# Windowed attention on TensorE: two windows' scores in one product, attention and transposes cut into other runs, new orders on all engines

## The chip, the cores and the metric

One core of a Trainium2 chip. The metric is the device time of one execution in microseconds; the median of three runs stands for the kernel. The profile is one further look at one execution.

The engines in the profile's words: PE is TensorE's matmul and PEld its weight load, DVE is VectorE, ACT ScalarE, POOL GpSimd, SPq the queue that issues the DMAs.

## The reference, cut to what matters

A cross attention over x and a context (32 batches of 128 tokens of 128), then a stack of six layers, each with windowed attention and a gated feed-forward. Per layer and batch, in fp32:

```python
qkv = x @ Wqkv                      # 128 x 3072, x with half its features shifted by one token
q, k = l2norm(q) * qs, l2norm(k) * ksc   # 16 heads of 64
q = q * cos * scale + rotate_half(q) * sin * scale
k = k * cos * inv + rotate_half(k) * sin * inv
# 4 windows of 32 queries; window w sees the keys of windows w-1 and w
sim = jnp.where(mask, -big, einsum('bhwie,bhwje->bhwij', bq, bk2) * 8)
out = softmax(sim) @ bv2
x = x + out @ Wo
xn = layernorm(shifted x); a, gate = split(xn @ W1 + b1)
x = x + (a * gelu(gate)) @ W2 + b2
```

## The kernel before, in words

A unit is one batch in one layer: 192 units, numbered layer by layer. The cross attention runs first, in 32 slots of its own (`xslot`). Then each engine runs the same `slot(n, k)` for n = -2, -1, ... 196, most of them in a loop of two slots per pass. In one slot an engine handles parts of several units: `part(n, lag)` gives unit n - lag. The order of the calls at the end of each engine's `slot` is the order in which that engine works; between engines there are only semaphores. So the slots overlap as in a pipeline, and the time of one slot is the time per unit.

TensorE's slot is written out at the end of the kernel: `attn_out` (L1363), `ffn_out` (L1351), a projection of queries and keys (`proj_qk`, L1252), `transpose_qk` (L1290), `transpose_z` (L1377), two projections, `transpose_P` (L1270), `scores` (mask L1314, products L1322), `attend` (L1339), `transpose_zn` (L1383), `proj_v` (L1262), `ffn_gate` (L1392), `ffn_a` (L1400), and two projections of the next and this unit.

Where an operand has fewer than 128 rows or an output fewer than 128 partitions, matmuls use a part of the array, a tile, and several tiles work side by side:

- `transpose_qk`: 64 transposes of 32 tokens x 128 features, four row tiles.
- `transpose_P`: 16 transposes of 64 tokens x 128, two row tiles.
- `scores`: 8 pairs of heads x 4 windows x 2 heads = 64 products of 32 queries with 64 keys (64 rows x 32 columns of the array, 64 columns streamed), on eight tiles (2 by head, 4 by window).
- `attend`: for 4 head groups, three windows of queries (64, 32 and 32 wide), 2 halves and 2 heads: 48 products on four tiles of 64 x 64. Values stand shifted in three copies (`vs`), made by three DMAs per half (`shift_v`).

An fp32 product is two matmul instructions in the trace, each with a weight load; a transpose is one.

ScalarE copies PSUM to SBUF (`copy_T`, `copy_PT`, `copy_o`, `copy_v`), squares the projections, and takes exponentials and gelu, with two table loads a slot. VectorE multiplies by the rotary tables (`rotary`, L963 and L966), sums squares, refines the inverse root, does maximum, subtraction and row sums of the softmax, and the statistics and the normalising step of the layer norm (`norm_apply`, L1030). GpSimd adds the rotary halves, multiplies by the norms and the softmax's factors, and does the layer norm's power. At the first unit of each layer, the new weights are loaded by the same DMA queue that shifts the values and `zm`.

## Time and profile before

| | us |
|---|---|
| median of 3 runs | 3308.11 |
| lowest and highest | 3307.62, 3310.73 |
| span of the profiled execution | 3304.7 |
| TensorE busy | 3125.4 |
| VectorE busy | 2884.0 |
| ScalarE busy | 2663.4 |
| GpSimd busy | 2447.9 |
| TensorE busy in the first 400 us (cross attention and first slots) | 297.3 |
| TensorE busy from 400 to 3200 us | 2750.5 |
| TensorE busy from 3200 us to the end | 77.6 |

The profile counts an engine busy from the start of an instruction to its end, overlapping ones once. The start of a matmul is read from the record, its end is modelled (about 0.22 us after the start in the tiled runs); how long a run of matmuls holds TensorE is therefore read from its first start to the first start of what follows.

### The profile page before, as it was taken

What the parts mean: (1) busy time and instruction counts of PE and PEld (TensorE: products, weight loads), DVE (VectorE), ACT (ScalarE), POOL (GpSimd) and SP (SyncE); (2) the same over time, 40 slices, a digit from 0 to 9 for tenths busy, and PEclk for the clock granted to TensorE, in tenths of its full rate; (3) what the DMA queues carried; (4) which work ended last, traced back from release to release, by engine and by line L of the source; (5) the groups of instructions that cost most, each with busy time, mean ns of one, the idle gap of its engine ahead of it and who ended that gap; (6) DMA issues with size and microseconds to landing.
All of it is one profiled execution on the core that took longest, in us unless ns stands there. A gap on an engine that the chain in (4) does not pass through costs nothing.

```text
span 3304.7 us, 181505 instructions
## 1 busy us (share of the span) xinstructions
PE 3125.4 (95%) x71268; PEld 2192.5 (66%) x71268; DVE 2884.0 (87%) x6045; ACT 2663.4 (81%) x5440; POOL 2447.9 (74%) x2673
## 2 busy tenths in 40 slices
PE   6776899999999999999999999999999999999996
PEld 4443567676667676676767667676676767667665
DVE  7886789999899999899999899998899999899984
ACT  6886678888788888788888788888788888788874
POOL 3333778888788888788888778787787878788883
PEclk9988999999999999999999999999999999999997
DMA  3000112122222222222222212122221212212121
GB/s 79 8 7 10 47 51 59 50 59 71 67 56 53 56 53 77 63 54 55 54 55 74 68 50 59 50 59 77 57 59 50 59 50 77 66 50 59 50 58 50
DMA packets 150374, 182.24 MB, mean 55 GB/s; under 512 B 51572, under 2 KB 74162, under 8 KB 149554
## 3 DMA queue, kind: packets, MB, share of 16 engines
q1 hardware_dynamic: 150322, 181.55, 21.2%
q8 instruction: 33, 0.54, 0.1%
q14 instruction: 19, 0.16, 0.0%
HBM read 21.32 MB, written 2.10 MB: 7 GB/s over the span
## 4 chain that ended last, share of the span: by engine, by line
PE 57%; issue 13%; DVE 10%; ACT 10%; POOL 5%; SPq 1%; DVEq 1%; DMA 1%; ACTq 1%; POOLq 0%
PE bank L1252 13%; PE bank L1339 8%; PE bank L1322 7%; PE bank L1262 5%; PE bank L1363 5%; PE bank L1270 3%; PE bank L1290 3%; ACT L798 3%; DVE tb L966 3%; ACT P L774 3%; PE bank L1392 2%; ACT gl L766 2%; POOL qk L524 2%; DVE bank L1075 2%; PE bank L1400 2%
## 5 line engine op out<-in xcount | busy, mean ns | idle before, releaser
L533 POOL TENSOR_TENSOR qk<-qk,rn 128x512 f32<-128x512 f32 x768 | 803.0, 1046 | 356.8 <-DVE rn L985 356.8
L524 POOL TENSOR_TENSOR qk<-ta,tb 128x512 f32<-128x512 f32 x768 | 978.6, 1274 | 2.5 <-DVE tb L966 2.5
L1252 PE MATMUL bank<-wqkv,zsT 128*128 128x512 f32 x1536 | 819.9, 617 | 25.4 <-ACT vt L705 12.3
L963 DVE TENSOR_TENSOR ta<-bank,rot 128x512 f32<-128x512 f32 x768 | 527.5, 687 | 116.1 <-ACT sq L688 87.4
L966 DVE TENSOR_TENSOR tb<-bank,rot 128x512 f32<-128x512 f32 x768 | 523.0, 681 | 0.0
L1068 DVE TENSOR_REDUCE bank<-sq 128x32 f32<-128x2048 f32 x192 | 440.6, 2295 | 25.1
L688 ACT ACTIVATE sq<-bank 128x512 f32<-128x512 f32 x768 | 445.2, 611 | 14.8 <-PE bank L1252 12.1
L696 ACT ACTIVATE qkT<-bank 128x512 f32<-128x512 f32 x768 | 396.6, 602 | 57.1 <-PE bank L1290 56.9
L1363 PEld LDWEIGHTS bank<-wo,oT 128*128 128x128 f32 x3072 | 375.4, 193 | 92.4 <-issue 92.4
L743 ACT ACTIVATE znT<-bank,small 128x128 f32<-128x128 f32 x192 | 87.9, 458 | 431.8 <-PE bank L1383 431.8
L564 POOL TENSOR_TENSOR P<-P,rowsum 128x512 f32<-128x512 f32 x384 | 392.9, 1045 | 20.0 <-DVE rowsum L1083 20.0
L1262 PE MATMUL bank<-wqkv,zsT 128*128 128x512 f32 x768 | 399.8, 603 | 1.2 <-DVE tb L966 1.1
L1363 PE MATMUL bank<-wo,oT 128*128 128x128 f32 x3072 | 376.6, 276 | 0.5 <-ACT gl L766 0.5
L1252 PEld LDWEIGHTS bank<-wqkv,zsT 128*128 128x128 f32 x1536 | 238.0, 195 | 193.1 <-DVE tb L966 170.2
L1290 PEld LDWEIGHTS bank<-cst,qk 32*128 32x128 f32 x12288 | 212.5, 137 | 172.9 <-issue 172.9
L1339 PE MATMUL bank<-PT,vs 64*64 64x32 f32 (+1 forms) x18432 | 310.9, 220 | 11.3 <-issue 11.3
L1339 PEld LDWEIGHTS bank<-PT,vs 64*64 64x64 f32 x18432 | 291.4, 135 | 30.0 <-issue 12.3
L539 POOL TENSOR_TENSOR rstd<-ve,half_neg 128x1 f32<-128x1 f32 x192 | 105.8, 551 | 254.5 <-DVE ve L1023 254.5
L1075 DVE TENSOR_REDUCE bank<-P 128x16 f32<-128x1024 f32 x192 | 235.8, 1228 | 66.7 <-ACT P L774 66.6
L1322 PEld LDWEIGHTS bank<-qkT 64*32 64x32 f32 x24576 | 278.1, 105 | 14.1 <-issue 3.9
L1322 PE MATMUL bank<-qkT 64*32 64x64 f32 x24576 | 281.7, 225 | 3.0 <-issue 3.0
L1290 PE MATMUL bank<-cst,qk 32*128 32x32 f32 x12288 | 228.5, 223 | 21.0 <-DVE rowsum L1083 2.9
(131 smaller groups left out, 5740.6 us busy)
## 6 DMA issues: line engine op xcount, KB each, us to landing
vs<-vt SPq DMA_DIRECT2D x1152, 128.0 KB, 2.4
wqkv<-L_ffn_Wqkv SPq DMA_DIRECT2D x6, 1024.0 KB, 5.0
zm<-zm SPq DMA_DIRECT2D x192, 31.8 KB
wqkv<-L_ffn_Wqkv SPq DMA_DIRECT2D x6, 512.0 KB, 3.7
wo<-L_ffn_Wo SPq DMA_DIRECT2D x6, 512.0 KB, 4.0
z_sb<-x SPq DMA_DIRECT2D x4, 512.0 KB, 5.1
ctxb<-ctx SPq DMA_DIRECT2D x32, 64.0 KB, 1.8
w<-L_ffn_W SPq DMA_DIRECT2D x6, 341.0 KB
```

Of the source, the lines that this page charges most:

```text
L524: g.tensor_tensor(o, i0, i1, ALU.add).then_inc(s["g_add"], 1)
L533: g.tensor_tensor(q3, q3, r3, ALU.mult).then_inc(s["g_qk"], 1)
L688: a_.activation(sq[:, 512 * j:512 * j + 512], bank[j % 2][:, :], ACT.Square)\
L963: v_.tensor_tensor(ta[:, c].rearrange("p (h d) -> p h d", d=DH), bank[j % 2][:, :].rearrange("p (h d) -> p h d", d=DH), rot[:, o:o + 64].u ...
L966: v_.tensor_tensor(tb[:, c].rearrange("p (h c d) -> p h c d", c=2, d=32)[:, :, ::-1, :], bank[j % 2][:, :].rearrange("p (h c d) -> p h c d ...
L1068: v_.tensor_reduce(sm, sq[:, :].rearrange("p (h d) -> p h d", d=DH), AX.X, ALU.add)\
L1252: t_.matmul(bank[j % 2][:, :], zsT[:, pu, :], wqkv[:, 512 * j:512 * j + 512], start=True, stop=True).then_inc(s["p_qk"], 1)
L1262: t_.matmul(bank[r][:, :], zsT[:, k % 2, :], wv[:, :, r, :], start=True, stop=True)\
L1290: ins = t_.transpose(TB[t][:, 32 * p:32 * p + 32], qk[tok, pb, 128 * p:128 * p + 128], ident[tok, tok])
L1322: ins = t_.matmul(SC[e][32 * w:32 * w + 32, 64 * p:64 * p + 64], qkT[dr, p, 32 * w:32 * w + 32], qkT[dr, PAIRS + p, k0:k0 + 64], start=Fal ...
L1339: ins = t_.matmul(bank[4 + r][64 * e:64 * e + 64, 128 * i + q0:128 * i + q0 + nq], vs[kr, pc, w, hc:hc + 64], PT[kr, 4 * e + i, q0:q0 + nq ...
L1363: ins = t_.matmul(bank[7][:, 384:512], oT[:, p, :], wo[:, 2 * (p % 4) + p // 4, :], start=p == 0, stop=p == PAIRS - 1)
```

## The change

- A product of the scores covers windows 0 and 1 together (64 queries, the same 64 keys) on two tiles; windows 2 and 3 keep 32-query products, on four tiles, with window 2's two halves of keys in reversed order. The mask is widened for that reversed order. 48 products in place of 64.
- The scores run in two parts: mask and windows 2 and 3; later windows 0 and 1.
- Attention times values: two sets of key rows in place of three. One run of 16 products is 96 queries wide, the other 64 wide and adds to the same banks; the transposed weights stand in PTA and PTC, with a factor of 0 or 1 per partition (`C_HALF`) where only half the keys count. 32 products in place of 48. The two runs stand in different slots. `vs` has two copies, so two DMAs per half.
- Queries and keys are transposed in 64-row tiles, in two runs of 16 (keys to banks 2 and 3, queries to banks 4 and 5).
- ScalarE copies the transposed weights in four pieces in place of two.
- The statistics of the norms (`sm`, `n0`, `n1`, `rs`) stand in SBUF in place of PSUM. The layer norm's small add and its normalising step go from VectorE to GpSimd.
- Each engine has a new order of the same parts, with other lags: the projections of queries and keys one slot before the unit's values, scores at lag 1, softmax and attention at 2 and 3, the feed-forward at 4. Each part has a semaphore of its own. Inside the loop only the waits that others don't imply are kept (`edge` waits stand outside the loop alone).

```diff
+    c[:, C_MASK + 64:C_MASK + 96] = c[:, C_MASK + 32:C_MASK + 64]
+    c[:, C_MASK + 96:C_MASK + 128] = c[:, C_MASK:C_MASK + 32]
+    c[:, C_HALF] = (r // WIN) % 2
+    c[:, C_HALF + 1] = 1 - (r // WIN) % 2
...
-        PT = sb("PT", [128, PAIRS, S])
+        PTA = sb("PTA", [128, PAIRS, 3 * WIN])
+        PTC = sb("PTC", [128, PAIRS, 2 * WIN])
         vt = sb("vt", [128, 2, 2, INNER // 2])
-        vs = sb("vs", [128, 2, 3, INNER // 2])
+        vs = sb("vs", [128, 2, 2, INNER // 2])
...
+        sm = sb("sm", [128, 2 * HEADS])
+        n0 = sb("n0", [128, 2 * HEADS])
+        n1 = sb("n1", [128, 2 * HEADS])
+        tiny = sb("tiny", [128, 2 * HEADS])
+        eps = sb("eps", [128, 1])
+        rs = sb("rs", [128, HEADS])
...
+        def done(unit, total=UNITS):
+
+            return min(max(unit + 1, 0), total) if isinstance(unit, int) else unit + 1
+
+        def unit(n, k, lag, total=UNITS):
+
+            u = n - lag
+            return u, (not isinstance(u, int)) or 0 <= u < total, (k - lag) % 2
 
...
+                for r in (0, 1):
+
+                    wait(sp, f"a_v{r}", done(u))
                     wait(sp, "p_AV", count(2, u - 2, 2))
                     rows = slice(64 * r, 64 * r + 64)
-                    for j in range(3):
-                        sp.dma_start(vs[rows, par, j, :], vt[32 * j:32 * j + 64, par, r, :]).then_inc(s[f"l_v{par}"], 16)
+                    for j in range(2):
+                        sp.dma_start(vs[rows, par, j, :], vt[64 * j:64 * j + 64, par, r, :]).then_inc(s[f"l_v{par}"], 16)
...
+                u, on, p = unit(n, k, 3)
+                if on:
+                    wait(pool, "d_agg", done(u))
+                    g.tensor_tensor(ve[:, p:p + 1], mv[:, 1:2], eps[:, 0:1], ALU.add).then_inc(s["g_ve"], 1)
+                    wait(pool, "g_ve", done(u))
+                    g.tensor_tensor(rstd[:, p:p + 1], ve[:, p:p + 1], half_neg[:, 0:1], ALU.pow).then_inc(s["g_rstd"], 1)
+
+                u, on, p = unit(n, k, 3)
+                if on:
+                    wait(pool, "g_rstd", done(u))
+                    edge(pool, u, "p_znT", done(u - 1))
+                    pool.nop(nofuse=True)
+                    g.tensor_scalar(zn[:, :], zm[:, p, 0:2, :].rearrange("p c e -> p (c e)"), mv[:, 0:1], rstd[:, p:p + 1],
+                                    ALU.subtract, ALU.mult).then_inc(s["d_zn"], 1)
+
...
+                    a_.activation(PTA[:, :, 0:64], bank[4][:, :].rearrange("p (h q) -> p h q", h=PAIRS), ACT.Copy).then_inc(s["a_PA0"], 1)
...
+                    a_.activation(PTC[:, :, 0:32], bank[5][:, :].rearrange("p (h q) -> p h q", h=PAIRS)[:, :, 0:32], ACT.Copy, scale=cst[:, C_HALF + 1:C_HALF + 2]).then_inc(s["a_PC0"], 1)
...
+                    a_.activation(PTC[:, :, 32:64], bank[5][:, :].rearrange("p (h q) -> p h q", h=PAIRS)[:, :, 32:64], ACT.Copy).then_inc(s["a_PC1"], 1)
...
+                    a_.activation(PTA[:, :, 64:96], bank[5][:, :].rearrange("p (h q) -> p h q", h=PAIRS)[:, :, 0:32], ACT.Copy, scale=cst[:, C_HALF:C_HALF + 1]).then_inc(s["a_PA1"], 1)
...
-                        for p in range(2 * PAIRS):
-                            for t in range(4):
-                                tok = slice(32 * t, 32 * t + 32)
-                                ins = t_.transpose(TB[t][:, 32 * p:32 * p + 32], qk[tok, pb, 128 * p:128 * p + 128],
-                                                   ident[tok, tok])
-                                if p == 2 * PAIRS - 1:
...
-                            for w, (q0, nq) in enumerate(((0, 64), (64, 32), (96, 32))):
-                                for r in range(2):
-                                    for e in range(2):
-                                        kr = slice(64 * r, 64 * r + 64)
-                                        hc = 128 * i + 64 * e
-                                        ins = t_.matmul(bank[4 + r][64 * e:64 * e + 64, 128 * i + q0:128 * i + q0 + nq],
-                                                        vs[kr, pc, w, hc:hc + 64], PT[kr, 4 * e + i, q0:q0 + nq],
-                                                        start=True, stop=True)
...
-                attn_out()
-                ffn_out()
-                proj_qk(1)
-                transpose_qk()
-                transpose_z()
-                proj_qk(2)
-                proj_qk(3)
-                transpose_P()
-                scores()
-                attend()
-                transpose_zn()
-                proj_v(0)
-                ffn_gate()
-                ffn_a()
-                proj_qk(0)
-                proj_v(1)
...
+                    wait(pe, "p_AV0", done(u))
...
+                    pe.nop(nofuse=True)
+                    for i in range(4):
+                        for r in range(2):
+                            for e in range(2):
+                                kr = slice(64 * r, 64 * r + 64)
+                                hc = 128 * i + 64 * e
+                                ins = t_.matmul(bank[4 + r][64 * e:64 * e + 64, 128 * i + 64:128 * i + 128],
+                                                vs[kr, p, 1, hc:hc + 64], PTC[kr, 4 * e + i, :],
+                                                start=False, stop=True, skip_group_check=True)
+                        if i % 2 == 1:
+                            ins.then_inc(s["p_AV"], 1)
...
+                u, on, p = unit(n, k, 1)
+                if on:
+                    wait(pe, "g_qk2", done(u))
+                    wait(pe, "d_sub1", done(u - 1))
+                    edge(pe, u, "g_qk3", done(u))
+                    edge(pe, u, "d_sub0", done(u - 1))
+                    if isinstance(u, int) and u == 0:
+                        pe.wait_ge(s["x_x1"], B)
+                    pe.nop(nofuse=True)
+                    for c in range(PAIRS):
                         for t in range(2):
                             tok = slice(64 * t, 64 * t + 64)
...
+                            ins = t_.transpose(bank[2 + t][:, 64 * c:64 * c + 64],
+                                               qk[tok, p, 1024 + 128 * c:1152 + 128 * c], ident[tok, tok])
+                    ins.then_inc(s["p_trk"], 1)
...
+                    wait(pe, "g_qk0", done(u))
...
+                    pe.nop(nofuse=True)
+                    for c in range(PAIRS):
+                        for t in range(2):
+                            tok = slice(64 * t, 64 * t + 64)
+                            ins = t_.transpose(bank[4 + t][:, 64 * c:64 * c + 64],
+                                               qk[tok, p, 0 + 128 * c:128 + 128 * c], ident[tok, tok])
...
+                if on:
+                    wait(pe, "a_tr1", done(u))
+                    edge(pe, u, "a_tr2", done(u))
+                    edge(pe, u, "a_tr3", done(u))
+                    pe.nop(nofuse=True)
+                    for w in range(4):
+                        for e in range(2):
+                            dr = slice(64 * e, 64 * e + 64)
+                            i = 32 * min(w, 1)
+                            o = 64 if w == 2 else 0
+                            t_.matmul(SC[e][32 * w:32 * w + 32, :], selb[dr, i:i + 32],
+                                      maskb[dr, o:o + 64].unsqueeze(1).to_broadcast([64, PAIRS, DH]),
+                                      start=True, stop=False, skip_group_check=True)
...
+                    for c in range(PAIRS):
+                        for w in range(2, 4):
...
+                                kb = qkT[dr, PAIRS + c, 32 * w - 32:32 * w + 32].rearrange("p (t c) -> p t c", t=2)
+                                ins = t_.matmul(SC[e][32 * w:32 * w + 32, 64 * c:64 * c + 64],
+                                                qkT[dr, c, 32 * w:32 * w + 32], kb[:, ::-1, :] if w == 2 else kb,
+                                                start=False, stop=c == PAIRS - 1, skip_group_check=True)
+                    ins.then_inc(s["p_S23"], 1)
...
+                    wait(pe, "p_S23", done(u))
+                    edge(pe, u, "a_tr0", done(u))
+                    pe.nop(nofuse=True)
+                    for c in range(PAIRS):
+                        for e in range(2):
+                            dr = slice(64 * e, 64 * e + 64)
+                            ins = t_.matmul(SC[e][0:64, 64 * c:64 * c + 64], qkT[dr, c, 0:64], qkT[dr, PAIRS + c, 0:64],
+                                            start=False, stop=c == PAIRS - 1, skip_group_check=True)
+                    ins.then_inc(s["p_S"], 1)
...
+                    wait(pe, "a_PA1", done(u))
...
+                    pe.nop(nofuse=True)
+                    for i in range(4):
+                        for r in range(2):
+                            for e in range(2):
+                                kr = slice(64 * r, 64 * r + 64)
+                                hc = 128 * i + 64 * e
+                                ins = t_.matmul(bank[4 + r][64 * e:64 * e + 64, 128 * i + 0:128 * i + 96],
+                                                vs[kr, p, 0, hc:hc + 64], PTA[kr, 4 * e + i, :],
+                                                start=i == 0, stop=False, skip_group_check=True)
+                    ins.then_inc(s["p_AV0"], 1)
```

The new order on TensorE (lag in brackets): transpose of z (-1), transpose of zn (4), attend's 64-wide part (3), values 0 (0), gate (4), values 1 (0), projection 0 (-1), output (3), key transposes (1), query transposes (1), projection 1 (-1), feed-forward a (4), mask and windows 2 and 3 (1), projection 2 (-1), transposes of P (2), feed-forward out (4), projection 3 (-1), windows 0 and 1 (1), attend's 96-wide part (2).

## Rows read from the trace of the kernel before

**Rows 1.** The page: busy time, share of the span and instructions of each engine.

```profile
PE 3125.4 (95%) x71268; PEld 2192.5 (66%) x71268; DVE 2884.0 (87%) x6045; ACT 2663.4 (81%) x5440; POOL 2447.9 (74%) x2673
```

**Rows 2.** Stretches: length, busy us (instructions) of PE, PEld, DVE, ACT, POOL, clock, DMA.

```profile
1500.00:2000.00 500.00, 491.44 (x11878) 348.95 (x11877) 449.59 (x923) 415.34 (x824) 401.03 (x428) 1.00 0.23 60
```

**Rows 3.** Waits from 1000 to 3000 us: total us, times, longest us.

```profile
PEld bank L1252 <- DVE tb L966: 114.9, 131, 1.1
...
DVE stats L1009 <- DMA zm<-zm: 54.4, 127, 4.9
```

**Rows 4.** TensorE in order of time: start us, length us, operation.

```profile
1521.70 1.18 PE L1290 MATMUL bank<-cst,qk 32*128 32x32 f32 x64
1522.81 0.33 PE L1377 MATMUL bank<-cst,zcur 128*128 128x128 f32 x1
1522.98 2.18 PE L1252 MATMUL bank<-wqkv,zsT 128*128 128x512 f32 x4
1525.09 0.71 PE L1270 MATMUL bank<-cst,P 64*128 64x64 f32 x16
1525.73 0.41 PE L1314 MATMUL bank<-maskb,selb 64*32 64x512 bf16 x8
1525.95 1.46 PE L1322 MATMUL bank<-qkT 64*32 64x64 f32 x128
1527.35 1.60 PE L1339 MATMUL bank<-PT,vs 64*64 64x64 f32 x96
1528.88 0.33 PE L1383 MATMUL bank<-cst,zn 128*128 128x128 f32 x1
1529.05 1.02 PE L1262 MATMUL bank<-wqkv,zsT 128*128 128x512 f32 x2
...
1532.23 1.02 PE L1262 MATMUL bank<-wqkv,zsT 128*128 128x512 f32 x2
1533.09 1.95 PE L1363 MATMUL bank<-wo,oT 128*128 128x128 f32 x16
...
1535.54 1.02 PE L1252 MATMUL bank<-wqkv,zsT 128*128 128x512 f32 x2
1536.63 0.38 PE L1290 MATMUL bank<-cst,qk 32*128 32x32 f32 x12
```

**Rows 5.** Stretches, L1339 alone: x counts its matmuls begun by the end.

```profile
1527.34:1527.44 0.10, 0.09 (x4) 1.00 0.00 0
1527.34:1527.49 0.15, 0.14 (x8) 1.00 0.00 0
1527.34:1527.79 0.45, 0.44 (x28) 1.00 0.00 0
1527.34:1527.84 0.50, 0.49 (x32) 1.00 0.00 0
1527.34:1528.74 1.40, 1.39 (x96) 1.00 0.00 0
```

**Rows 6.** The same for L1222 in cross attention, 128*32 tiles, 512 columns.

```profile
202.80:202.84 0.04, 0.03 (x4) 1.00 0.00 0
202.80:203.26 0.46, 0.45 (x4) 1.00 0.00 0
202.80:203.29 0.49, 0.48 (x8) 1.00 0.00 0
```

**Rows 7.** Groups of instructions, 1000 to 3000 us: busy us, mean ns.

```profile
L721 ACT ACTIVATE PT<-bank 128x512 f32<-128x512 f32 x262 | 142.5, 597 | 8.2
...
L1030 DVE TENSOR_SCALAR zn<-zm,mv,rstd 128x128 f32<-128x128 f32 x131 | 79.9, 610 | 0.0
...
L548 POOL TENSOR_TENSOR zmb<-zm,b2r 128x128 f32<-128x128 f32 x132 | 60.7, 460 | 0.0
L743 ACT ACTIVATE znT<-bank,small 128x128 f32<-128x128 f32 x131 | 60.0, 458 | 280.1 <-PE bank L1383 280.1
...
L733 ACT ACTIVATE zsT<-bank 64x128 f32<-64x128 f32 x131 | 34.6, 264 | 0.0
```

918 lines of the change are left out of this document (479 added, 439 removed), and 4 rows, old and new, of the table names.

## The prediction

> **What bounds the kernel now.** I read the page's busy shares first, then a table of the steady stage by stretch, then the list of waits, then TensorE alone in order of time through one slot. The page gives TensorE 95% of the span [rows 1]. The layers run from about 400 to 3200 us; in 500 us of that stage TensorE is busy 491.4, VectorE 449.6, ScalarE 415.3 and GpSimd 401.0 us (of a slot of 15.0: 14.8, 13.5, 12.5 and 12.05), at a granted clock of 1.00, which is the 2.4 GHz level [rows 2]. The long waits of the other engines are waits for their turn; the waits of TensorE itself are short: its loads of the projections wait for the rotary products 114.9 us in 131 slots, most of it behind matmuls [rows 3]. So the slot is TensorE's own sequence. It takes 15.0 us (14.93 in [rows 4], from the start of L1290 at 1521.70 to 1536.63), and there are 192 units, some 190 slots at full pace. What is left of the 3308 us (cross attention, ramp, drain) is hardly touched. The measure is the median, 3308.1; the profiled span is 3304.7, so 3.4 us lie around it.
>
> Whatever is added to TensorE's sequence therefore counts 190 times, and what is taken from VectorE counts nothing as long as TensorE has work.
>
> **What the tiled runs cost TensorE now.** Full-array matmuls (projections, output, feed-forward) are the same before and after, so I sum only the rest, from one start to the next [rows 4]. A projection takes 0.86 us from its start to the next (1532.23 to 1533.09). From L1252 at 1535.54 to L1290 at 1536.63 are 1.09, so 0.23 lie between a projection and the transposes. Queries and keys (64 instructions) 1.11; the input's transpose 0.17; the two projections after it take 2.11 where 1.72 stream, so 0.39, of which I put 0.10 to entering the tiled run and 0.29 to the wait for the rotary product; transposes of P 0.64; mask 0.22; scores (128 instructions) 1.40; attend (96) 1.53; the transpose of zn 0.17. Tiled work and its seams: 0.23 + 1.11 + 0.17 + 0.10 + 0.64 + 0.22 + 1.40 + 1.53 + 0.17 = 5.57 us. That wait of 0.29, 0.1 of the 0.23 and about 0.1 elsewhere in the slot are what a better order can win.
>
> **What sets the pace of a tiled run.** An fp32 product is two instructions that stream its columns twice each. In attend there are four tiles of 64x64. Counting records that began by a given time [rows 5]: four by 1527.44, eight by 1527.49, 28 by 1527.79, 32 by 1527.84, all 96 by 1528.74. The first set begins at 1527.35 [rows 4], the second after 1527.44: some 0.09 us for 64 columns streamed twice (0.053 us at 2.4 GHz). Over the run a set of four takes 1.40/24 = 0.058. The same lag stands in cross attention: four column tiles with 512 columns begin by 202.84, the next four between 203.26 and 203.29, so about 0.45 where 0.43 (half a projection) stream [rows 6]. So the second instruction of a product on its tile comes 0.03 us late, and a product of N columns costs its tile about N/600 + 0.035 us: 0.142 for N = 64, 0.195 for N = 96. Scores check this: eight products per tile, 8 x 0.142 = 1.14, in a run of 1.40 that pays about 0.17 to fill and empty. What counts is thus how many products lie one behind the other on a tile, not how many instructions there are.
>
> **The change on TensorE, per slot.**
> - Scores. Windows 2 and 3: 32 products on four tiles, 8 deep: 1.14 (bounds 0.85, streaming alone, to 1.23, the 1.40 of [rows 4] less 0.17). Windows 0 and 1: 16 products with 64 query rows on two tiles, again 8 deep: 1.14 (0.85 to 1.33, if 64-column loads came on top). Before, all windows lay side by side on eight tiles, 8 deep once. The instructions fall from 128 to 96, the depth doubles.
> - Attend. With 96 columns: 4 deep, 0.79 (0.67 to 0.80). With 64 columns: 4 deep, 0.58 (0.47 to 0.60). Together 1.37 against 1.36 (1.53 less 0.17): nothing won, since fewer weight loads are paid with 640 instead of 512 columns per tile.
> - Transposes. 16 instructions take 0.64 for 64-row tiles [rows 4]; two such runs joined pay the seam once: 1.11, as now. The mask stays 0.22.
> - Seams. The tiled work was two blocks (queries/keys; P, mask, scores, attend) and is five: attend's rest; transposes; mask and windows 2, 3; P; windows 0, 1 and attend's first part. Entering costs 0.10 and filling and emptying 0.17. Five entries and five and a half fills: 1.44, against 2 x 0.10 + 4 x 0.17 = 0.88 before.
>
> The sum after: transposes of z and zn back to back 0.28; attend's rest 0.10 + 0.17 + 0.58 = 0.85; query and key transposes 0.10 + 1.11 = 1.21; mask and windows 2, 3 0.10 + 0.22 + 0.17 + 1.14 = 1.63; P 0.74; windows 0, 1 0.10 + 0.17 + 1.14 = 1.41; attend's first part 0.79 + 0.1 = 0.89. Total 7.01, so +1.44. Bounds: 5.9 with the lower ends and half the new seams, 7.3 with the upper ends. The other way go the stalls, 0.4 to 0.5 a slot (0.1 if the new order has its own). Net +1.0 (-0.1 to +1.6).
>
> TensorE also waits for itself: attend's rest for the first part, across two transposes of 0.28 us, and windows 0, 1 for windows 2, 3, which lie 3 us back. With the first everything on its queue stands; records of attend last 0.22 us, so at most 0.1, inside the range.
>
> On the seams the Trainium skill, TensorEngine Tiling (Array Packing), Key Properties, says that changing the tiling mode drains TensorE. It gives no price; the trace agrees, with 0.23 and 0.10 us of entry, and it speaks against splitting.
>
> **The other engines, per slot.** ScalarE: two copies of 512 columns become one and three of 256; a copy of 512 columns takes 0.60, one of 128 takes 0.26, and one of 128 with scale and bias 0.46 [rows 7], so 0.35 to 0.55 each. Busy 12.5 becomes 13.0 to 13.4. VectorE loses the normalising step (0.61) and a small add, 13.5 becomes 12.8; statistics in SBUF instead of PSUM I put at nothing, on a covered engine. GpSimd gets both: between the 0.46 of an add of that size and the 0.61 that VectorE took [rows 7], I take 0.5, with 0.3 for the small add; 12.05 becomes 12.9, at worst 14. None reaches 16. I walked the four orders once round with these durations: the projections' waits for rotary products go (0.5 to 1 us of slack), the scores' wait for the last query copy and the output projection's wait for gelu are left with 0.1 to 0.4. New waits on GpSimd sit at the variance: zn, four normalisations and next slot's adds queue behind it, with 1 us to spare. Two of three shift DMAs per half stay (four, not six); nobody waits for them.
>
> At each of five layer borders bn_stats waits, before the change, up to 4.9 us for its shift DMA [rows 3], and TensorE stands behind it. A longer slot hides a part, though the shift is now queued behind the load of w1 and its wait: -2 a border, -10. The depth falls by one slot of drain: another -10. Both may be nothing.
>
> **Result.** 3308 + 190 x 1.0 - 20 = 3478; I say 3475.
>
> **Rivals.**
> - A, the count sets the pace. If issuing bounded the tiled runs (1.40/128 = 0.011 and 1.53/96 = 0.016 us each), 96 and 64 instructions would save 0.35 + 0.51 and give back 0.56 in seams; with the stalls gone TensorE needs 14.3 (15.0 - 0.4 - 0.86 + 0.56), VectorE and GpSimd follow closely: 14.4 a slot, 3308 - 114 - 20 = 3175. For it: fewer instructions. Against: sets begin 0.09 apart and then bunch, and cross attention's 4 tiles take column time. 10%. The Trainium skill, TensorE: Matmul & The Clock Gate, Part 1, gives a floor of about 25 ns from start to start, which would favour this change more (64 instructions fewer, 1.6 us a slot); the trace's 11 ns says that it does not hold across tiles.
> - B, pure streaming. With fewer tiles in flight the 0.03 lag vanishes: scores 1.80, attend 1.1, half the new seams: 14.9 to 15.2 a slot, 3270 to 3340. 14%.
> - C, a new wait. GpSimd's zn or the last key or query copy comes late, TensorE waits 0.6 to 1.5 a slot more: 16.6 to 17.5, 3590 to 3750. For it: slack of 0.1 at the scores' wait. 14%.
> - That the change does nothing can't be: TensorE's sequence is another.
>
> **How the numbers follow.** Forecast (slot 15.4 to 16.5) 62%, A 10, B 14, C 14. The range takes in B and the lower edge of C and leaves out A and most of C: 3290 to 3600. Faster: A and half of B, 17%; within 0.2%, which is about what a measurement of this kernel can tell from no change, 3%; slower 80%.
>
> **What would show it.** A slot of about 16.0 us between two transposes of z, with TensorE still over 95% busy; windows 2, 3 and windows 0, 1 each over 1.1 us from first to last start; the two parts of attend 0.85 and 0.9; no wait for rotary products. Wrong if the score runs take 0.9 or less each, if seams cost nothing, or if TensorE shows waits of over 0.5 us a slot.

## The result and the profile after

The changed kernel takes 3344.05 us (median of 4 runs, 3341.65 to 3345.25) against 3307.86 of the kernel before beside it: a ratio of 1.0112, with an interval of 1.0098 to 1.0126. It is 1.1% slower: the direction is the forecast's, but the growth is 36 us where 167 were expected (3475 less 3308).

The page's busy shares, the counterpart of [rows 1]:

```profile
PE 3225.3 (96%) x52836; PEld 2286.5 (68%) x52836; DVE 2758.6 (83%) x5661; ACT 2822.0 (84%) x5827; POOL 2637.3 (79%) x3060
```

TensorE runs a quarter fewer instructions (52836 against 71268) and is busy 100 us longer. The layers' stretch in the table by stretches (length; busy us and instructions of PE, PEld, DVE, ACT, POOL; clock, DMA share, GB/s):

```profile
400.00:3200.00 2800.00, 2796.34 (x47665) 2007.00 (x47663) 2351.44 (x4699) 2421.67 (x4876) 2376.99 (x2707) 1.00 0.17 41
```

TensorE's own waits from 400 to 3250 us (total us, times, longest us), all that the view lists:

```profile
PE bank L1321 <- POOL zn L565: 3.4, 5, 1.0
PE bank L1373 <- DMA wqkv<-L_ffn_Wqkv: 0.2, 1, 0.2
```

TensorE is all but without idle time. The five waits at L1321 are those at the five layer borders; between the borders every wait of the old order is gone, and the slot is nothing but TensorE's own sequence, at a granted clock of 1.00. That sequence in order of time (start us, length us; the ends are modelled, so read from one start to the next; left out are two projections, the transposes of zn and of the queries, and the rest of the last two runs), from one transpose of z to the next, the counterpart of [rows 4]:

```profile
1511.07 0.33 PE L1315 MATMUL bank<-cst,zcur 128*128 128x128 f32 x1
...
1511.44 0.69 PE L1337 MATMUL bank<-PTC,vs 64*64 64x64 f32 x32
1512.06 1.13 PE L1348 MATMUL bank<-wqkv,zsT 128*128 128x512 f32 x2
1513.03 0.83 PE L1356 MATMUL bank<-znT,w 128*128 128x128 f32 x6
...
1515.41 1.95 PE L1383 MATMUL bank<-wo,oT 128*128 128x128 f32 x16
1517.29 0.71 PE L1398 MATMUL bank<-cst,qk 64*128 64x64 f32 x16
...
1518.43 1.13 PE L1425 MATMUL bank<-wqkv,zsT 128*128 128x512 f32 x2
1519.39 0.82 PE L1432 MATMUL bank<-znT,w 128*128 128x128 f32 x6
1520.14 0.41 PE L1446 MATMUL bank<-maskb,selb 64*32 64x512 bf16 x8
1520.38 1.06 PE L1454 MATMUL bank<-qkT 64*32 64x64 f32 x64
1521.38 1.13 PE L1464 MATMUL bank<-wqkv,zsT 128*128 128x512 f32 x2
1522.43 0.71 PE L1478 MATMUL bank<-cst,P 64*128 64x64 f32 x16
1523.07 0.94 PE L1486 MATMUL bank<-w,hT 128*128 128x128 f32 x6
1523.85 1.02 PE L1494 MATMUL bank<-wqkv,zsT 128*128 128x512 f32 x2
1524.80 1.08 PE L1504 MATMUL bank<-qkT 64*64 64x64 f32 x29
1525.67 0.29 PE L1521 MATMUL bank<-PTA,vs 64*64 64x96 f32 x1
...
1526.54 0.33 PE L1315 MATMUL bank<-cst,zcur 128*128 128x128 f32 x1
```

The slot is 15.47 us. From 900 to 1280 us, between two layer borders, the starts of VectorE's aggregation (one a slot, L1110 after, L1017 before) lie 15.48 apart on average, before the change 15.03. Full-array work takes the same 8.92 in both (projections 0.86 each, output 1.78, the three products of the feed-forward 0.66 or 0.67 each). The tiled work and its seams take the rest, 6.55, against 5.57 before. A seam shows in the neighbour: a projection behind a tiled run takes 0.96 to 0.97 from its start to the next (1512.06 to 1513.03) where an undisturbed one takes 0.86, and a full-array step ahead of a run 0.09 or 0.10 more as well.

Where the 38.6 us of the span (3343.3 against 3304.7) come from, by those starts: 191 gaps of 15.034 and 15.483 (the same means, unrounded) give 86 more. The borders, the first slots and the drain give 45 back: all 191 gaps together are 2914.7 before, 43 above 191 x 15.034, and 2955.3 after, 2 below 191 x 15.483. Of the 45, some 25 are the five borders, 7 the first five slots and 14 the last five. The ends of the span account for the last 2. One border, before and then after, VectorE in order of time (the border's own gap is the first of the two in each fence):

```profile
852.18 0.18 DVE L1017 BATCH_NORM_AGGREGATE mv<-stats 128x2 f32<-128x6 f32 x1
871.15 0.18 DVE L1017 BATCH_NORM_AGGREGATE mv<-stats 128x2 f32<-128x6 f32 x1
886.66 0.18 DVE L1017 BATCH_NORM_AGGREGATE mv<-stats 128x2 f32<-128x6 f32 x1
```

```profile
855.53 0.17 DVE L1110 BATCH_NORM_AGGREGATE mv<-stats 128x2 f32<-128x6 f32 x1
873.22 0.17 DVE L1110 BATCH_NORM_AGGREGATE mv<-stats 128x2 f32<-128x6 f32 x1
887.69 0.17 DVE L1110 BATCH_NORM_AGGREGATE mv<-stats 128x2 f32<-128x6 f32 x1
```

Before, 18.97 and 15.51 (and 16.00 ahead of them) are 5.4 above three usual gaps. After, 17.69 (and 15.82 ahead of it) is followed by 14.47, and then 14.79: of the 2.5 that this border costs, 1.7 are made up within two slots, in which VectorE, late by its wait, catches up with TensorE. So the engines other than TensorE can run at 14.5 a slot.

At this border the old kernel loses its time in two ways. TensorE waits 3.57 us for zn (L1383, 18.4 us at the five borders together), and right behind that wait its granted clock falls to 0.50, the 1.2 GHz level:

```profile
874.48 0.33 PE L1383 MATMUL bank<-cst,zn 128*128 128x128 f32 x1 [3.57 <-DVE zn L1030]
875.50:878.80 3.30, 3.30 (x14) 3.19 (x14) 3.17 (x4) 2.95 (x7) 3.30 (x5) 0.50 0.11 33
```

The four pieces of work from 874.69 to 879.50 take 4.81 instead of 3.18 at a clock of 1.00, so 1.6 of the 5.4 are the clock. The trace has such a stretch, of 3.4 or 6.8 us, at each of the five borders before the change, in or right behind L1383's wait of 3.6 to 3.8, and none between 400 and 3200 us after it, where TensorE waits at most 1.0. (The page rounds the clock of both kernels to 1.00 over these 2800 us.)

### The profile page after: what moved, and what is told of

Read it like the earlier page. It is cut to its first block and busy times, and to the rows that moved or that the text cites. A ratio compares the mean times of both kernels' runs of the same rounds, so it can differ in the third digit from the quotient of the medians.

```text
span 3343.3 us, 134060 instructions
## 1 busy us (share of the span) xinstructions
PE 3225.3 (96%) x52836; PEld 2286.5 (68%) x52836; DVE 2758.6 (83%) x5661; ACT 2822.0 (84%) x5827; POOL 2637.3 (79%) x3060
## 5 line engine op out<-in xcount | busy, mean ns | idle before, releaser
L1383 PEld LDWEIGHTS bank<-wo,oT 128*128 128x128 f32 x3072 | 374.5, 192 | 94.8 <-issue 89.2
L1179 DVE TENSOR_REDUCE sm<-sq 128x32 f32<-128x2048 f32 x192 | 436.9, 2276 | 0.0
L1383 PE MATMUL bank<-wo,oT 128*128 128x128 f32 x3072 | 376.1, 276 | 3.2 <-ACT gl L768 3.1
L539 POOL TENSOR_TENSOR P<-P,rowsum 128x512 f32<-128x512 f32 x192 | 200.1, 1042 | 217.8 <-DVE rowsum L1047 217.8
L1025 DVE TENSOR_REDUCE rs<-P 128x16 f32<-128x1024 f32 x192 | 234.2, 1220 | 127.0 <-ACT P L779 127.0
L1135 DVE TENSOR_REDUCE rowmax<-bank 128x8 f32<-128x512 f32 x192 | 132.7, 691 | 235.2 <-PE bank L1504 235.2
L1504 PEld LDWEIGHTS bank<-qkT 64*64 64x64 f32 x6144 | 194.1, 134 | 144.3 <-issue 144.1
L1504 PE MATMUL bank<-qkT 64*64 64x64 f32 x6144 | 220.5, 221 | 0.0
L1464 PE MATMUL bank<-wqkv,zsT 128*128 128x512 f32 x384 | 216.9, 647 | 1.8 <-DVE tb L1057 1.8
L1348 PE MATMUL bank<-wqkv,zsT 128*128 128x512 f32 x384 | 217.6, 649 | 0.0
L1425 PE MATMUL bank<-wqkv,zsT 128*128 128x512 f32 x384 | 216.4, 646 | 0.3 <-ACT vt L785 0.3
L1356 PEld LDWEIGHTS bank<-znT,w 128*128 128x128 f32 (+1 forms) x1152 | 151.9, 180 | 91.3 <-issue 67.5
L1432 PEld LDWEIGHTS bank<-znT,w 128*128 128x128 f32 (+1 forms) x1152 | 152.0, 180 | 89.6 <-issue 89.5
L1068 DVE SCALAR_TENSOR_TENSOR hT<-bank,small,gl 128x128 f32<-128x128 f32 (+1 forms) x576 | 165.7, 343 | 57.2 <-PE bank L1432 57.1
L1478 PEld LDWEIGHTS bank<-cst,P 64*128 64x128 f32 x3072 | 110.6, 139 | 148.8 <-issue 148.8
```

Of the source, the lines that this page charges most:

```text
L1025: v_.tensor_reduce(rs[:, :], P[:, p, :].rearrange("p (h t) -> p h t", t=DH), AX.X, ALU.add).then_inc(s["d_sum"], 1)
L1179: v_.tensor_reduce(sm[:, :], sq[:, :].rearrange("p (h d) -> p h d", d=DH), AX.X, ALU.add).then_inc(s["d_sumsq"], 1)
L1348: t_.matmul(bank[0][:, :], zsT[:, p, :], wv[:, :, 0, :], start=True, stop=True).then_inc(s["p_v0"], 1)
L1383: ins = t_.matmul(bank[7][:, 384:512], oT[:, c, :], wo[:, 2 * (c % 4) + c // 4, :], start=c == 0, stop=c == PAIRS - 1)
L1464: t_.matmul(bank[0][:, :], zsT[:, p, :], wqkv[:, 1024:1536], start=True, stop=True).then_inc(s["p_qk2"], 1)
L1504: ins = t_.matmul(SC[e][0:64, 64 * c:64 * c + 64], qkT[dr, c, 0:64], qkT[dr, PAIRS + c, 0:64], start=False, stop=c == PAIRS - 1, skip_grou ...
```

## The experiments

The theory after the result: the pace of a tiled run is set by the longest of three things, not by depth x (N/600 + 0.035). These are issuing the instructions, streaming the columns on a tile, and loading a tile's weights. (Depth is the number of products that lie one behind the other on a tile; a seam is the change between full-array work and a tiled run.) The rivals: depth alone (the prediction's rule), or a price of each seam that hides the rest. The edits are to TensorE's part alone, except in the two on DMA order. Slots are means from 900 to 1280 us. Where no interval is given, the time is that of one run, beside a median of 3308.3 (e3, e4), 3305.2 (e6 to e8) or 3307.9 (e9) for the kernel before.

**e1: all scores in one run, at the place of the mask.**

```diff
-                        for w in range(2, 4):
+                        for w in range(4):
...
-                    ins.then_inc(s["p_S23"], 1)
+                    ins.then_inc(s["p_S"], 1)
...
-                    wait(pe, "p_S23", done(u))
-                    edge(pe, u, "a_tr0", done(u))
-                    pe.nop(nofuse=True)
-                    for c in range(PAIRS):
```

> The changed kernel with all scores again in one run of 128 instructions on eight tiles, in the place of the mask and windows 2 and 3; windows 0 and 1 are 32-query products again. In the changed kernel the two score runs take 1.00 and 0.87 us from start to start and two seams of about 0.1 more. Theory (a run takes the longest of streaming one tile's columns, loading weights, and 0.0096 us per instruction): the joined run takes 1.40 as in the kernel before, the slot falls from 15.47 by 0.6 to 0.7 to about 14.8 us, 3344 falls to about 3215, if the other engines keep up. Rival (the split was free, the extra time is in the seams of attend and transposes): the slot falls by less than 0.3, time above 3290. Rival (another engine is next in line): TensorE shows waits, 3240 to 3300.

Measured: 3321.8 us, 1.0036 of the kernel before (1.0022 to 1.0050), 22 under the changed kernel; slot 15.27. TensorE in order of time:

```profile
1512.75 0.83 PE L1432 MATMUL bank<-znT,w 128*128 128x128 f32 x6
1513.73 0.41 PE L1447 MATMUL bank<-maskb,selb 64*32 64x512 bf16 x8 [0.15 <-ACT qkT L820]
1513.95 1.46 PE L1456 MATMUL bank<-qkT 64*32 64x64 f32 x128
1515.33 1.12 PE L1466 MATMUL bank<-wqkv,zsT 128*128 128x512 f32 x2
```

The joined run takes 1.38 where the parts took 1.00 + 0.87, so by the starts the split costs 0.49 (and 0.05 more in attend, whose first products start among the last of windows 0 and 1: it takes 0.87 behind them and 0.82 here). Only 0.2 of the slot arrives. The mask now needs all four copies and comes 0.23 later (0.98 behind L1432 instead of 0.75), with its wait for ScalarE's last query copy in the row. And projection 3, now the neighbour of attend alone, takes 1.08 to the next start instead of 0.95. What is saved (0.54, and 0.03 in the mask) less these two (0.36) is the 0.2.

**e2: attend in one run, the 64-wide part right behind the 96-wide one.**

```diff
+                u, on, p = unit(n, k, 2)
+                if on:
...
+                    edge(pe, u, "a_PC1", done(u))
...
+                                ins = t_.matmul(bank[4 + r][64 * e:64 * e + 64, 128 * i + 64:128 * i + 128],
+                                                vs[kr, p, 1, hc:hc + 64], PTC[kr, 4 * e + i, :],
+                                                start=False, stop=True, skip_group_check=True)
```

> The changed kernel with the 64-wide part of attend directly behind the 96-wide part, in place of two transposes and half a slot border later; nothing else. Theory (a seam between full array and tiles costs about 0.1 on entry and 0.1 on exit, and a run loses 0.05 at its first set): the slot falls by 0.2 to 0.25 us to 15.25, the time to about 3300. Rival (the seams are hidden or the wait of TensorE for its own first part is the cost): less than 0.1, above 3325, or the joined run is longer by what the separate one was.

Measured: 3374.7 us, 1.0200 (1.0182 to 1.0217); slot 15.67. A miss: 0.2 longer instead of shorter. TensorE:

```profile
1505.93 0.69 PE L1518 MATMUL bank<-PTC,vs 64*64 64x64 f32 x32
...
1507.06 1.12 PE L1328 MATMUL bank<-wqkv,zsT 128*128 128x512 f32 x2
1508.22 0.93 PE L1336 MATMUL bank<-znT,w 128*128 128x128 f32 x6
```

The 64-wide part between the transpose of zn and the gate was the cover for ScalarE's copy of zn. Without it the step from values 0 to the gate takes 1.16 instead of 0.97, the gate's weight loads wait for that copy up to 1.0 us (0.2 in the changed kernel), and the gate itself takes 0.76 instead of 0.66. The part takes 0.74 here instead of 0.62. A seam was saved, a cover lost.

**e3 and e4: half the columns streamed in the scores, in the changed kernel and in the one before** (half the keys are left out; the instructions and their weights stay).

```diff
-                                ins = t_.matmul(SC[e][32 * w:32 * w + 32, 64 * c:64 * c + 64],
-                                                qkT[dr, c, 32 * w:32 * w + 32], kb[:, ::-1, :] if w == 2 else kb,
+                                ins = t_.matmul(SC[e][32 * w:32 * w + 32, 64 * c:64 * c + 32],
+                                                qkT[dr, c, 32 * w:32 * w + 32], qkT[dr, PAIRS + c, 32 * w:32 * w + 32],
...
-                            ins = t_.matmul(SC[e][0:64, 64 * c:64 * c + 64], qkT[dr, c, 0:64], qkT[dr, PAIRS + c, 0:64],
+                            ins = t_.matmul(SC[e][0:64, 64 * c:64 * c + 32], qkT[dr, c, 0:64], qkT[dr, PAIRS + c, 0:32],
```

> The changed kernel with 32 instead of 64 columns streamed in every product of the scores, so half of the keys are left out; instructions and weight loads are the same in number. Theory (both score runs are bound by streaming): windows 0 and 1 fall from 0.87 to about 0.50, windows 2 and 3 from 1.00 to about 0.75 (then bound by loads or instructions at 0.038 a set of four). Rival (bound by the number of instructions or by loads): both stay.

> The kernel before with 32 instead of 64 columns streamed in every product of the scores, so half of the keys are left out. Theory (128 instructions at 0.0096 us bound this run on eight tiles): it stays at 1.40 us from start to start. Rival (my prediction's rule, two instructions of a product stream one behind the other and the second 0.035 us late): it falls to 8 x 0.09 + 0.17 = 0.9 us.

Measured: e3 3278.9 us, slot 15.15; e4 3287.1, slot 14.93. In e3 windows 2 and 3 fall from 1.00 to 0.69, and windows 0 and 1 stay (0.85 against 0.87). In e4 the run falls only from 1.40 to 1.26. The pace shows when the matmuls begun by a given time are counted (x, in stretches from a run's start), first windows 2 and 3 of the changed kernel, then of e3, then windows 0 and 1 of the changed kernel, then the scores of e4:

```profile
1520.37:1520.68 0.31, 0.29 (x24) 1.00 0.08 18
1520.37:1521.13 0.76, 0.74 (x56) 1.00 0.08 18
```

```profile
1507.91:1508.21 0.30, 0.29 (x34) 1.00 0.08 18
1507.91:1508.48 0.57, 0.56 (x64) 1.00 0.08 18
```

```profile
1524.79:1525.10 0.31, 0.30 (x10) 1.00 0.00 0
1524.79:1525.69 0.90, 0.89 (x30) 1.00 0.00 0
```

```profile
1500.68:1500.93 0.25, 0.24 (x29) 1.00 0.00 0
1500.68:1501.26 0.58, 0.57 (x69) 1.00 0.00 0
```

- Windows 2 and 3, 64 columns: 32 instructions in 0.45, so 0.056 for four, one on each tile. That is 64 columns streamed twice (0.053 at 2.4 GHz), with no 0.03 on every second one.
- With 32 columns: 30 in 0.27, 0.036 for four, 9.0 ns each. Streaming would be 0.027. The load of 32 columns of weights (0.032, e8) and the issuing rate (8.3 ns, so 0.033 for four, e4) both lie near; which of them takes over isn't told apart here.
- Windows 0 and 1: 20 in 0.59, 0.059 for a pair, and the whole run the same length with half the columns. So it isn't streaming here.
- Scores of e4: 40 in 0.33, 8.3 ns each, for a set of eight 0.066, where streaming and the load would need 0.03. So it is neither of these, and is taken as the rate of issuing. The same run with its 64 columns takes 1.40 and not 1.26: 10 ns each.
- Those 10 ns aren't even. Counted the same way in the scores of [rows 4], from 1525.95: 40 have begun by 1526.34, 55 by 1526.47, 74 by 1526.67, 89 by 1526.79. So stretches at the issuing rate (15 in 0.13, 15 in 0.12) change with slower ones (19 in 0.20); once in 32 instructions, several starts lie 16 to 26 ns apart. Why is open.

**e8: windows 0 and 1 with 32 columns of weights** (three quarters of their scores are left out).

```diff
-                            ins = t_.matmul(SC[e][0:64, 64 * c:64 * c + 64], qkT[dr, c, 0:64], qkT[dr, PAIRS + c, 0:64],
+                            ins = t_.matmul(SC[e][0:32, 64 * c:64 * c + 32], qkT[dr, c, 0:32], qkT[dr, PAIRS + c, 0:32],
```

> The changed kernel with 32 instead of 64 queries and 32 instead of 64 keys in the products of windows 0 and 1 (three quarters of these scores are left out); windows 2 and 3 as they were. In the experiment with half the keys this run did not fall (0.85 for 0.87). Theory (loading 64 columns takes a tile 0.056 us, as long as streaming 64 keys): with 32 columns to load and 32 to stream the run falls to about 0.5 us or less. Rival (a fixed interval of 0.056 per instruction on one tile): it stays at 0.85.

Measured: 3289.0 us, slot 15.18. The run of 32 falls to 0.62 (1500.54 to 1501.16). The same count:

```profile
1500.53:1500.70 0.17, 0.17 (x10) 1.00 0.00 0
1500.53:1501.05 0.52, 0.52 (x32) 1.00 0.00 0
```

22 instructions in 0.35: 0.032 for a pair. Half the columns left it at 0.059, half the columns and half the weight width brings it to 0.032, so the load of 64 columns of weights was the pace. (The output of a product narrows with its weights, from 64 partitions to 32; the runs can't tell the two apart.) The Trainium skill, TensorE: Matmul & The Clock Gate, LDWEIGHTS (loading the stationary operand), gives a load as the number of weight columns over 1.2 in ns, whatever the rows: as estimates, 53 for 64 and 27 for 32. The trace agrees to within 6 ns (0.059 and 0.032), and attend's four tiles, a set in 0.058 [rows 5], fit as well, though each set loads four tiles: the loads of different tiles run side by side. The transposes don't follow this rule of the Trainium skill, by which a load of 128 columns would take 107 as an estimate: in L1398, 16 instructions load 128 columns each, eight on either of two tiles, and begin within 0.49, so one about every 0.062 on a tile. The price of a load is shown here for the products alone.

**e9: the kernel before with its scores split in two, back to back.**

```diff
-                            for w in range(4):
+                            for w in range(2, 4):
...
+                        for p in range(PAIRS):
+                            for e in range(2):
+                                dr = slice(64 * e, 64 * e + 64)
+                                ins = t_.matmul(SC[e][0:64, 64 * p:64 * p + 64], qkT[dr, p, 0:64], qkT[dr, PAIRS + p, 0:64],
+                                                start=False, stop=p == PAIRS - 1, skip_group_check=True)
```

> The kernel before with one part of the change alone: windows 2 and 3 as 64 instructions, then windows 0 and 1 as 64-query products in 32 instructions, directly behind each other in the place of the scores. Theory: 16 x 0.056 + 16 x 0.058 and one change of tile shape (0.15 in the experiment with alternating shapes) against 1.40: the run takes 1.95 to 2.0, slot 15.05 + 0.5 to 0.6, about 3410 us. Rival (fewer instructions are cheaper, 96 against 128 at 0.0096): the run falls below 1.2, time below 3290.

Measured: 3383.7 us, slot 15.55, 0.52 more than before. TensorE:

```profile
1521.83 1.06 PE L1322 MATMUL bank<-qkT 64*32 64x64 f32 x64
1522.82 1.09 PE L1328 MATMUL bank<-qkT 64*64 64x64 f32 x30
1523.69 0.28 PE L1344 MATMUL bank<-PT,vs 64*64 64x64 f32 x2
```

0.99 + 0.87 = 1.86 against 1.40 for the 128 instructions of [rows 4], and attend, which starts among the last of them, takes 1.60 instead of 1.53. So the larger products of windows 0 and 1 cost 0.46 by the starts and 0.52 with what attend loses, in the old order, with no new seam and no new wait (the change of tile shape that lay between scores and attend now lies between the two parts of the scores). Alone in the old kernel this part of the change costs 76 us (0.52 x 191 is 99; the gaps together grow by only 82, since the borders cost less beside longer slots).

**e6: 64-wide and 32-wide tiles alternating within the scores.**

```diff
                     for c in range(PAIRS):
+                        for e in range(2):
+                            dr = slice(64 * e, 64 * e + 64)
+                            t_.matmul(SC[e][0:64, 64 * c:64 * c + 64], qkT[dr, c, 0:64], qkT[dr, PAIRS + c, 0:64],
...
+                        for w in range(2, 4):
```

> As the previous kernel, but windows 0 and 1 stay 64-query products, interleaved pair by pair with windows 2 and 3: 96 instructions that alternate between 64x64 and 64x32 tiles. Theory (a tile is paced by streaming or loading 0.056 a set, and different tile shapes run side by side): the run takes 16 x 0.058 + 0.13 = 1.05 instead of 1.38 and the slot falls by another 0.3. Rival (a change of tile shape drains TensorE each time, 16 changes of about 0.1): the run takes 2.0 to 3.0 us.

Measured: 3758.3 us, slot 17.61. The run takes 4.06 (1510.36 to 1514.42) in 16 pieces, of which the first two are:

```profile
1510.36 0.33 PE L1490 MATMUL bank<-qkT 64*64 64x64 f32 x4
1510.62 0.32 PE L1496 MATMUL bank<-qkT 64*32 64x64 f32 x8
...
```

A piece lasts 0.255 on average, and its work (two instructions on each tile) is two times 0.057, so a change of tile shape costs 0.14 here. The Trainium skill, TensorEngine Tiling (Array Packing), Key Properties, says that changing the mode drains the engine; here it has its price.

**e7: one more seam** (projection 1 moved between key and query transposes).

```diff
+                u, on, p = unit(n, k, -1)
+                if on:
+                    wait(pe, "a_v1", done(u - 1))
...
+                    t_.matmul(bank[1][:, :], zsT[:, p, :], wqkv[:, 512:1024], start=True, stop=True).then_inc(s["p_qk1"], 1)
```

> The changed kernel with one projection moved between the key and the query transposes, so that these are two separate runs; nothing else. Theory (a seam costs about 0.10 before and 0.10 after a run): from the first key transpose to what follows the query run 0.15 to 0.25 us more than 0.55 + 0.59 + 0.96; beside it the scores may wait 0.2 to 0.5 for the last query copy, which is visible as a gap before the mask. Rival (seams are free, the gaps seen are modelled ends): no change in that sum.

Measured: 3407.6 us, slot 15.84, so +0.36 for the same instructions with one run more. From the key transposes to L1432 it is 2.35 (1508.70 to 1511.05) against 2.10 (1517.29 to 1519.39), and the step from there to the mask 0.86 against 0.75. No wait is in the trace there. A run of its own costs some 0.35: 0.15 because two runs of 16 transposes take longer than one of 32, 0.10 on the way in, 0.10 on the way out.

**e5: mask and all scores in one run, directly ahead of attend.** Both lessons together: the run of e1 on eight tiles, at the place of windows 0 and 1, where the last copy is long done and attend follows without a seam.

```diff
-                    wait(pe, "p_S23", done(u))
-                    edge(pe, u, "a_tr0", done(u))
+                    wait(pe, "a_tr0", done(u))
+                    edge(pe, u, "a_tr1", done(u))
+                    edge(pe, u, "a_tr2", done(u))
+                    edge(pe, u, "a_tr3", done(u))
...
+                    for w in range(4):
```

> The changed kernel with the mask and all scores in one run of 128 instructions on eight tiles (as in the first experiment), but in the place of windows 0 and 1, directly before attend's 96-wide part. In the first experiment the joined run took 1.38 instead of 1.00 + 0.87, but 0.23 went into a wait for the last copy of the queries and 0.13 into a seam before attend. Theory: here neither is paid and the seam of windows 2 and 3 goes too: slot 15.47 - 1.42 + 0.75 = 14.8 us, time 3344 - 0.67 x 191 = 3216. Rival (the engines behind have no slack below 15.0): TensorE shows waits of 0.2 to 0.5 a slot, 3250 to 3300, for instance on the row maxima's chain or on ScalarE.

Measured: 3241.1 us, 0.9805 (0.9787 to 0.9822); slot 14.83. TensorE:

```profile
1514.85 0.41 PE L1484 MATMUL bank<-maskb,selb 64*32 64x512 bf16 x8
1515.07 1.46 PE L1493 MATMUL bank<-qkT 64*32 64x64 f32 x128
1516.46 0.89 PE L1511 MATMUL bank<-PTA,vs 64*64 64x96 f32 x32
```

Moving the scores makes 1.0112 into 0.9805. Against the kernel before, 38 us of this are the slot (14.83 against 15.03), and some 30 the borders and the first and last slots. The slot is 0.65 shorter: 0.54 by the eight tiles (1.39 + 0.82 for scores and attend's first part instead of 0.99 + 1.74, and 0.01 in the mask), 0.09 by the way into the run that is gone. Its way out shows hardly a gain (projection 2 takes 1.04 instead of 1.06), so the ways in and out are worth 0.11 here, and not the 0.20 of e7.

**e10 and e11: the new layer's shift DMA ahead of the load of w1**, in the kernel before (e10) and in e5's (e11).

```diff
-                shift_z(start, 0)
+                if layer == 0:
+                    shift_z(start, 0)
...
                     shift_v(end + 2, 0)
+                    shift_z(end, 0)
                     load_w1(layer + 1)
```

> The kernel before with one DMA order changed: at each layer border the shift of zm for the first unit stands ahead of the load of w1 instead of behind it. Theory (TensorE's stall of 3.6 us at each of five borders, and the low clock behind it, come from bn_stats waiting for this shift): borders lose about 1 instead of 5.5 us, 3306 falls by 15 to 22 us. Rival (the other loads on the queue delay it as much, or w1 then comes late): within 5 us of before.

> The kernel of the fifth experiment (scores in one run before attend, 3241 us) with the same change of DMA order at the borders. Its slots of 14.83 over 191 units give 2832 us where 2847 lie between its first and last statistics, so 14 us are lost at borders and ramps. Theory: half of that comes back, 3241 falls by 5 to 10 us. Rival (its borders are bound by the load of the projections' weights): no change within 3 us.

Measured: e10 3301.2 us, 0.9977 (0.9967 to 0.9986), 7 gained where 15 to 22 were expected; e11 3234.2 us, 0.9778 (0.9761 to 0.9794), 7 under e5, though its interval and e5's overlap. In e10 the first border's gaps are 15.72, 18.01 and 14.40 instead of 16.00, 18.97 and 15.51. VectorE's longest wait for this DMA shrinks from 4.9 to 3.8, so most of it wasn't the queue behind w1. The clock stays at 1.00 behind this border, and still falls to 0.50 behind the other four. In e11 the gap at the border, 16.68 in e5, is 15.23, and the five borders together cost 8.6 less. But all 191 gaps together are only 1.6 less (2845.1 against 2846.7), since the first and last slots take longer. That the 7 us of e11 come from the borders is therefore not shown.

**e12: e5 with attend joined, values 1 ahead of the gate, and the transposes of queries and keys ahead of the output projection.**

```diff
+                    wait(pe, "d_rot3", done(u))
...
+                    t_.matmul(bank[1][:, :], zsT[:, p, :], wv[:, :, 1, :], start=True, stop=True).then_inc(s["p_v1"], 1)
...
+                u, on, p = unit(n, k, 3)
+                if on:
+                    wait(pe, "a_gelu", done(u - 1))
```

> The kernel of the fifth experiment with attend's two parts in one run again, as in the second experiment, but with the waits that this caused covered by other work: on TensorE both value projections now stand before the gate, and the transposes of keys and queries before the output projection. Theory (a seam is 0.15 to 0.35, and the second experiment lost it to an uncovered wait for zn's copy): slot 14.83 falls to 14.5 to 14.7, where the next engine stands (slots after a border run at 14.47), time 3180 to 3220. Rival (the cover fails: the output projection waits for gelu or the copies for the transposes come late): slot above 14.9, 3260 or more.

Measured: 3394.5 us, 1.0260 (1.0243 to 1.0277); slot 15.66. A miss of 0.8 a slot. TensorE at projection 2, then VectorE in the same slot:

```profile
1523.30 0.83 PE L1412 MATMUL bank<-znT,w 128*128 128x128 f32 x6
1524.66 1.13 PE L1420 MATMUL bank<-wqkv,zsT 128*128 128x512 f32 x2 [0.53 <-DVE tb L1057]
```

```profile
1521.68 1.22 DVE L1025 TENSOR_REDUCE rs<-P 128x16 f32<-128x1024 f32 x1 [1.63 <-ACT P L779]
...
1523.92 0.68 DVE L1057 TENSOR_TENSOR tb<-bank,rot 128x512 f32<-128x512 f32 x1
```

L1412 takes 1.36 to the next start instead of 0.66. Projection 2 waits for the rotary product, which VectorE does behind its sum, which waits 1.63 for ScalarE's exponential. That exponential stands on ScalarE behind the copies of z and zn, gelu and a table load, all of which start with the transpose of z. With attend joined ahead of z, TensorE needs 0.6 less from there to projection 2, but this chain needs the same. The gelu itself waits 0.23 for the gate, which stands behind values 1; in e5 it has no such wait. Which of the three edits weighs most wasn't taken apart.

## Why the prediction was right in sign and wrong in size

Point by point, the predicted terms and their measured lengths (with the seams that the timeline shows, from one start to the next):

| term | predicted | measured |
|---|---|---|
| transposes of z and zn | 0.28 | 0.37 |
| attend's rest | 0.85 | 0.73 |
| key and query transposes | 1.21 | 1.34 |
| mask, windows 2 and 3 | 1.63 | 1.43 |
| transposes of P | 0.74 | 0.84 |
| windows 0 and 1 | 1.41 | 0.96 |
| attend's first part | 0.89 | 0.87 |
| sum | 7.01 | 6.54 |

- **The step that failed: "a product of N columns costs its tile about N/600 + 0.035 us".** It gave each score run 1.14 on top of its seam, and over both 0.65 too much with the seams counted: 0.24 each by the rule, and the rest mostly because windows 0 and 1 pay no filling and emptying where attend follows on tiles of the same shape. By the prediction's own sign (each over 1.1 us from first to last start) it fails too: windows 2 and 3 take 0.85, windows 0 and 1 0.93. The 0.03 was read from one lag at the beginning of attend, before the stream is steady [rows 5], and from one between two sets of cross attention [rows 6]. Attend's 0.058 a set isn't streaming plus a lag: it is the load of 64 columns of weights (e3, e8). The check against the old scores (8 x 0.142 + 0.17 = 1.31, held to be near 1.40) was no support: their 10 ns an instruction lie near the issuing rate (8.3, e4), which the rule doesn't have. The steady pace is 0.056 an instruction on a tile for windows 2 and 3, and 0.059 for windows 0 and 1, so 0.9 for 16 on a tile and not 1.14.
- **The mechanism held:** what was saved in instructions was lost in depth, since two and four tiles did in two runs what eight did in one. The split costs 0.46 to 0.49 a slot by the starts, 0.52 to 0.54 with attend's share (e1, e9), over half of the growth of the tiled work. The rest is seams, less 0.09 that attend saves (0.82 + 0.62 for its two parts, 1.53 before). The 1.14 of the sum lies above, the 0.85 of its lower bound just below what was measured.
- **Seams** were taken as 0.10 in and 0.17 to fill and empty. The timeline has 0.09 to 0.10 in, about 0.10 out, and a first set some 0.1 late, and e7 prices a whole extra run at 0.35: a little over the 0.27. That is why three of the small terms came out 0.1 short (z, the transposes of queries and keys, those of P), which hid part of the error in the scores.
- **Stalls:** 0.4 to 0.5 expected back, 0.54 came (15.03 less 8.92 and 5.57), and no new wait took their place; rival C did not come.
- **Slot:** +1.0 expected, +0.45 measured: +0.97 of tiled work instead of +1.44, less 0.54. It is the low edge of the forecast's 15.4 to 16.5. Over 190 slots this makes 105 of the 131 us by which 3475 was too high (3344 measured).
- **Borders and drain:** -10 and -10 expected, -25 and -14 measured, and -7 in the first slots. Right in kind, too small. Two things were not in the sum: the two steps after a border run at 14.47 and 14.79 and make up for most of the wait, and the clock, which fell to 0.50 behind each border before the change, stays at 1.00.
- **Other engines:** VectorE 12.8 expected a slot, 13.0 measured (2351.4 of 2800 us at 15.48); ScalarE 13.4 against 13.0 to 13.4; GpSimd 13.1 against 12.9. GpSimd's normalising step was put at 0.5 and takes 0.80 (next section). None bounds the slot, as said.
- **Rival A** (the count sets the pace) fell for these runs: 96 score instructions take 1.87 where 128 took 1.40. It has a true core: on eight tiles issuing nearly binds. **Rival B** (pure streaming) was right on the pace of windows 2 and 3 and close in its 1.80 for both score runs (1.87), wrong on the seams and on attend.

What the change lost can be had back: with its waits gone and the scores whole again, next to attend, the same kernel is 2% faster than before (e5), and 2.2% with the DMA moved (e11, a gain over e5 that is not clear of the noise).

## What to carry to other kernels

Price a run of small tiles, here of fp32 products, as the longest of three: instructions times the issuing rate, and per tile the columns streamed and the weight columns loaded; merging products so that fewer tiles work side by side can take away instructions and still cost time. Take each term from the steady part of a run, not from its first sets, and count a way in and a way out for each run that stands alone. The old scores, at 10 ns an instruction, come out of this sum some 15% too short. Before moving a run to save a seam, look at which copy or chain its length was covering (e2, e12).

## What the runs showed of the hardware

- Over eight tiles, matmuls with a weight load each start every 8.3 ns (e4).
- A change of tile shape within a run costs 0.14 us (e6), an isolated run some 0.35 (e7).
- Weight loads of different tiles run side by side, and the load of 64 columns (0.059) binds where a tile streams no more than 64 columns, that of 32 is 0.032 (e3, e8). The transposes load 128 columns on a tile every 0.062 (L1398).
- In the layers, the granted clock fell to 0.50 at all five waits of TensorE of 3.6 to 3.8 us in the kernel before, and at four of the five of 2.6 to 2.7 in e10. At the waits of up to 1.0 us in the changed kernel it stayed at 1.00.
- The steady scores of the kernel before take 10 ns an instruction, more than the 8.3 of e4 and more than 64 columns streamed on eight tiles would ask. The rest falls in lags once in 32 instructions; their cause stays open.
- GpSimd's normalising step, two per-partition scalars on 128x128, takes 0.80 us where VectorE took 0.61 [rows 7], though a plain add of the same size takes GpSimd 0.46. The group from 1000 to 3000 us (busy us, mean ns, idle before it):

```profile
L565 POOL TENSOR_SCALAR zn<-zm,mv,rstd 128x128 f32<-128x128 f32 x129 | 102.9, 797 | 22.8 <-POOL rstd L558 22.8
```
